# One more wait on GpSimd: the two sums that make base2 are held until L_lo of the next graph is there

## The reference

```python
h = relu(layernorm(x))
A_hat = adj + I;  d = A_hat.sum(-1) ** -0.5
x = x + (A_hat * d[:, None] * d[None, :]) @ (h @ W + b)          # layer 0

h = relu(layernorm(x))                                           # layer 1
H = (adj != 0);  Dn = 1 / (H @ adj[0, :]);  Be = 1 / H.sum(0)
P = H @ diag(Be) @ H.T
t = relu(Dn * (P @ h) @ W1.T + b1)
t = layernorm(t) * gamma + beta                                  # 1024 wide
y = Dn * (P @ t) @ W2.T + b2
x = x + (y + h)
```

## Time and profile before

| What | Value |
|---|---|
| Median of 3 runs | 2405.9 us (2403.88 to 2405.99) |
| Span of the profiled execution | 2403.2 us |
| TensorE busy | 2211.9 us (92%) |
| VectorE busy | 2115.8 us (88%) |
| GpSimd busy | 1334.4 us (56%) |
| ScalarE busy | 1158.7 us (48%) |
| Chain that ended last | PE 56%, DVE 33%, issue 8% |

### The profile page before, as it was taken

How to read it: one execution, slowest core, us unless ns; L and a number is a source line. 1 busy time by engine, 2 the same in 40 slices (tenths; PEclk the granted TensorE clock), 3 DMA queues, 4 the chain that set the end, 5 groups by cost and what they waited for, 6 DMA issues and landing times.

```text
span 2403.2 us, 48798 instructions
## 1 busy us (share of the span) xinstructions
PE 2211.9 (92%) x14480; PEld 1799.3 (75%) x14480; DVE 2115.8 (88%) x4754; ACT 1158.7 (48%) x1809; POOL 1334.4 (56%) x2574
## 2 busy tenths in 40 slices
PE   6999999999999999999999999999999999999998
PEld 4777777777777777777777777777777777777776
DVE  6889888988898898889888988988898889888986
ACT  4444445454444444444444444444444454544443
POOL 3555555555555555555555555555555555555553
PEclk8999999999999999999999999999999999999999
DMA  3111111011111111111111111111111111111110
GB/s 134 34 37 33 38 39 33 33 39 37 33 33 39 37 33 36 40 33 33 39 38 33 33 39 37 33 33 40 36 33 38 38 33 33 39 37 33 33 37 19
DMA packets 76558, 90.39 MB, mean 38 GB/s; under 512 B 8576, under 2 KB 41344, under 8 KB 76544
## 3 DMA queue, kind: packets, MB, share of 16 engines
q1 hardware_dynamic: 76544, 90.22, 12.5%
HBM read 56.63 MB, written 33.55 MB: 38 GB/s over the span
## 4 chain that ended last, share of the span: by engine, by line
PE 56%; DVE 33%; issue 8%; DVEq 1%; ACT 0%; DMA 0%; POOL 0%; SPq 0%; POOLq 0%; ACTq 0%
PE ps_y L331 29%; PE ps_t L331 15%; DVE L_hi L712 7%; PE ps_t L306 5%; DVE L_lo L716 4%; DVE raw L667 4%; DVE x L664 4%; PE ps_t L308 4%; PE ps_t L307 4%; DVE hn_lo L728 3%; DVE h_lo L689 2%; DVE xh_lo L722 2%; DVE P_lo L694 1%; DVE H_T L703 1%; DVE ahat_T L701 1%
## 5 line engine op out<-in xcount | busy, mean ns | idle before, releaser
L762 POOL TENSOR_TENSOR base<-scr,x_t 128x512 f32<-128x512 f32 x128 | 165.7, 1294 | 706.6 <-ACT scr L474 706.6
L450 ACT ACTIVATE h<-z 128x512 f32<-128x512 f32 x256 | 161.8, 632 | 453.6 <-DVE z L641 453.6
L565 DVE BATCH_NORM_STATS2 raw<-h 128x6 f32<-128x512 f32 x256 | 177.8, 695 | 189.2 <-ACT h L450 189.2
L331 PE MATMUL ps_y<-w1h,t1h 128*128 128x512 f32 x1024 | 288.7, 404 | 0.7 <-ACT t1h L459 0.7
L331 PE MATMUL ps_y<-w1h,t1l 128*128 128x512 f32 x1024 | 275.2, 391 | 2.1 <-DVE t1l L582 2.1
L331 PE MATMUL ps_y<-w1l,t1h 128*128 128x512 f32 x1024 | 276.5, 392 | 0.0
L331 PE MATMUL ps_t<-w2h,t2h 128*128 128x512 f32 x1024 | 268.8, 405 | 1.1 <-ACT t2h L467 1.1
L331 PE MATMUL ps_t<-w2l,t2h 128*128 128x512 f32 x1024 | 266.7, 402 | 0.0
L459 ACT ACTIVATE t1h<-ps_t 128x512 fp32r<-128x512 f32 x128 | 76.4, 597 | 379.0 <-PE ps_t L308 379.0
L331 PE MATMUL ps_t<-w2h,t2l 128*128 128x512 f32 x1024 | 253.4, 390 | 0.0
L505 ACT ACTIVATE hn_hi<-h,sc 128x1024 f16<-128x1024 f32 x128 | 159.0, 1242 | 143.5 <-POOL sc L803 143.5
(11 more groups left out here) (117 smaller groups left out, 5998.8 us busy)
## 6 DMA issues: line engine op xcount, KB each, us to landing
x_t<-in_x_dram SPq DMA_DIRECT2D x128, 256.0 KB, 2.6
out_dram<-out_t SPq DMA_DIRECT2D x128, 256.0 KB, 2.0
adj_t<-in_adj_dram SPq DMA_DIRECT2D x128, 64.0 KB, 2.0
wrow_t<-in_adj_dram SPq DMA_DIRECT2D x128, 64.0 KB, 3.0
stage<-in_W1T_dram SPq DMA_DIRECT2D x1, 2048.0 KB, 11.6
stage<-in_W2T_dram SPq DMA_DIRECT2D x1, 2048.0 KB, 8.8
stage<-in_W_dram SPq DMA_DIRECT2D x1, 1024.0 KB, 8.5
b_all<-in_b_dram SPq DMA_DIRECT2D x2, 256.0 KB, 8.1
```

Source lines behind the costliest of these rows:

```text
L331: mm = pe.matmul(ps, t[:, j * 128:(j + 1) * 128], w[:, j, cols], start=(n == 0 and j == 0), stop=(n == 2 and j == blocks - 1))
L450: act.activation(h[:, cols], z[:, cols], ACT.Relu).then_inc(s_h[c], 1)
L565: dve.bn_stats(raw2[:, c, :], h[:, c * CH:(c + 1) * CH]).then_inc(s_raw2, 1)
L762: pool.tensor_tensor(base0[:, :], scr0[:, :], x_t[:, m, :], ALU.add).then_inc(s_base0, 1)
```

## The change

GpSimd gets a wait before sum2: it goes on only when s_lt shows that L_lo of graph p = k+1 has been written in the same step. In steps written out by hand the wait is left out where p is no graph any more (the last two c1 graphs). Nothing else is changed.

```diff
@@ -815,6 +815,8 @@
                     m = c1 % 2
 
                     wait(pool, s_psum2a, i, c1)
+                    if not isinstance(i, int) or p < NG:
+                        wait(pool, s_lt, i, p)
                     pool.tensor_tensor(sum2[:, :], scr2[:, :], b2_all[:, :], ALU.add).then_inc(s_psum2b, 1)
                     wait(pool, s_psum2b, i, c1)
                     wait(pool, s_vq, i, c1)
```

## The result

The changed kernel takes 2441.11 us (median of 4 runs, 2439.21 to 2442.65) against 2404.89 for the kernel before (4 runs, 2402.96 to 2405.99): a ratio of 1.0151, 95% interval 1.0137 to 1.0166. It is slower by 36 us, where 16 were forecast, and it lies 1 us outside the range. The sign was right, and so was the order in which the two engines take turns; two terms were too small.

The account below looks back on a forecast made before the run. TensorE and VectorE were taken to bound the kernel by turns. Half the steps 0.10 us later, half 0.16: 0.13 x 125 = 16 us, span 2419.4, plus the median's 2.7 offset: 2422 us, range 2405 to 2440.

Parts of the forecast that it names:

- What is held up: VectorE instructions blocked during GpSimd sums: L_hi and L_lo become short, xh_lo and hn_lo wait, hn_lo about 2.3 us.
- The freed 2.1 us: VectorE time per step released from L_hi and L_lo in A; most was to be idle, waiting for xh_hi.
- The order at the gap between xh_lo and hn_lo: base2 gets in ahead of hn_lo: xh_lo 0.55 behind sum2, base2 1.12 later, hn_lo 1.08 after that.
- Rival 1: VectorE keeps the port, hn_lo goes ahead of base2, t2 0.91 us earlier per step: 2292 us, chance 0.06.
- GpSimd's answer: Delay from a VectorE signal to GpSimd's start, taken as 0.08 us, so sum2 starts at +0.75 after L_hi starts.
- What TensorE gives back: At t2, TensorE was to absorb part of hn_lo's delay: 0.24 becomes 0.10 in A, 0.17 becomes 0.16 in B.
- A: One of two alternating step kinds (L_hi at 1211.63): hn_lo later by 0.24 us, t2 later by 0.10.
- B: The other alternating step kind (L_hi at 1230.04): hn_lo later by 0.17 us, t2 later by 0.16.
- nothing given back: Bound in which TensorE absorbs none of hn_lo's delay: 0.205 us per step, 26 us in all, 2432 us.
- VectorE's own path: VectorE's way to t2l and x1 starts 0.24 or 0.17 us later; no term was added for it.
- the clock: TensorE's granted clock stays at 1.00 (2.4 GHz); a fall to 1.2 GHz got chance 0.01 within the slower side.
- The advice of the Trainium skill: Scheduling the off-path engine: 268 us gain, down to 2138, if nothing replaced the freed blocks; chance 0.01.

Follow-up runs that it names:

- e1: The changed kernel with base2 also waiting for hn_lo of the same step, sum2 still waiting for L_lo: 2298.94 us, ratio 0.9557.
- e5: The changed kernel with sum2's wait moved from L_lo to L_hi: 2405.99 us, ratio 1.0001.
- e4: The changed kernel with TensorE's waits ahead of t2 reordered, t2l's first and those for hn_hi and hn_lo last: 2436.86 us, ratio 1.0130.
- e2: The changed kernel with both GpSimd sums waiting for hn_lo instead of L_lo: 2256.74 us, ratio 0.9381.
- e3: The kernel before with one added wait, for hn_lo, ahead of base2; sum2 not held: 2266.32 us, ratio 0.9422.
- e7: The kernel before with base2 alone waiting for L_lo, sum2 not held: 2406.79 us, ratio 1.0002.

## Why the prediction was right and wrong

- **What is held up, right.** L_hi 287 and L_lo 352 ns (forecast 0.28 and 0.35), idle time in front of xh_lo, base2 stretched to 1.55, hn_lo to 2.27. The freed 2.1 us became idle time and waiting, as said.
- **The order at the gap between xh_lo and hn_lo, right.** xh_lo 0.55 behind sum2, base2 1.13 behind xh_lo, hn_lo 1.08 behind base2: the three durations of the drain to 0.01. Rival 1 (VectorE keeps the port) is out. What it would have been worth was, in size, right too: e1 takes base2 out of that gap and ends at 2299.
- **GpSimd's answer, wrong: 0.08 should have been 0.14.** The prediction took it from bn_aggr and its add. Behind L_lo, L_hi, inv_t and hn_lo sum2 starts after 0.14 to 0.15 in every step read. With that sum2 ends at +2.10 instead of +2.04 and hn_lo comes 0.07 later: 0.07 x 125 = 9 us. e5 shows that this term counts in full.
- **What TensorE gives back, wrong.** "In A TensorE is itself just behind" failed. The earlier trace rows spoke against it already: there TensorE is idle for 0.28 in A, and what ends it is hn_lo. In the changed kernel TensorE was idle 1.51 us and still started 0.23 behind hn_lo. The prediction read a number that recurs in one kind of step as lateness, because t1 ended shortly before; the drain row, written out by hand, could not tell what is peculiar to the loop. e4 ties it to the order of the waits. A's term was to be 0.24 instead of 0.10, as the prediction itself had it for this case: 0.14 x 62 = 9 us.
- **The sum.** A: 4.86 + 0.23 - 4.55 - 0.24 = 0.30. B: 4.87 + 0.10 - 4.62 - 0.11 = 0.24. Mean 0.27 (the periods say 0.272), x 125 = 34, and 2 to 3 us from the ends. So 16 + 9 + 9 + 2.
- **The range, wrong by 1 us.** Its upper end took "nothing given back" with 0.05 for a later GpSimd. Both came true, with 0.07, and the ends of the kernel on top.
- **VectorE's own path and the clock.** No third term for VectorE, right: the periods are explained without one. The clock held at 1.00 in the steady steps, but was 0.50 in one stretch more of the drain, 1.6 us that the prediction did not have.
- **The advice of the Trainium skill (SBUF — State Buffer, section "Summary: rules for kernel authors") to schedule whichever is off the critical path, weighed at 0.01 as a gain from this change.** Rightly low for this place, yet the traces agree with the advice itself: e2 follows it by waiting until hn_lo is through, and is 149 us faster than before. The change waited for the wrong instruction.

## What to carry to other kernels

Two engines that exclude each other do not lose by a long overlapped instruction as such, but by what it delays on the chain: L_hi at 1.40 us cost less than 0.1 us a step, hn_lo at 2.28 cost 1.1. When work is held back from such an engine, follow it to where it lands, and hold it until the last instruction that the chain needs is through, not the first. Here a waiting GpSimd sum got in between two VectorE instructions that stand directly behind each other, so a queue without gaps was no protection.

## What the runs showed of the hardware that was not expected

- sum2 starts 0.14 to 0.15 us behind the end of L_lo, L_hi, inv_t (128x1) or hn_lo (128x1024), whichever it waits for, but base2 0.23 to 0.25 behind hn_lo (e1, e3) or L_lo (e7), and the small add 0.08 behind a bn_aggr. So the size of the result does not matter, and with the same producer the time differs by the GpSimd instruction that waits. base2 has other waits beside the one that counts; whether these make the difference was not tried.
- The time from hn_lo's end to the waiting product was 0.10 in one kind of step and 0.23 in the other with the wait for t2l written last, and 0.15 in both with it written first.
- With the same gaps ahead (0.98 and 1.38 us of idle before t1 and t2 in the drain), the granted clock of the 3.6 us from the start of t2 on was 1.00 in the kernel before and 0.53 in the changed one. What decides this is not shown; the lower level cost 1.6 us there.
